# Moving the gate and up weight loads of the expert stage from SyncE's queue to ScalarE's

## The reference

```python
# first half, x is [4, 8192, 1024], H = 2048
xn = rms_scale * x / (norm + EPS) * split_scale
K = sigmoid(xn @ W_K)
u, g_in, g_out = split(xn @ W_ugg, 3)
u = u * sigmoid(g_in) * (1.0 - K)
outputs = scan(h[t] = K[t-1] * h[t-1] + u[t])
x = layernorm(x + outputs * sigmoid(g_out) @ W_out + x)
# second half, per token, E = 8 experts, F = 768
scores = sigmoid(x @ W_gate_router); top 2, normalised to w
shared = silu(x @ Wg_s) * (x @ Wu_s) @ Wd_s
routed = sum over the two of w * (silu(x @ Wg[e]) * (x @ Wu[e])) @ Wd[e]
x = layernorm(x + shared + routed)
```

## Time and profile before

| | us |
|---|---|
| median of 2 runs | 6612.8 (6410.53 and 6815.06) |
| the profiled execution | 6211.95 |
| its span on the slowest core, 7 | 6210.1 |
| spans of all cores | 6129.4 to 6210.1 |
| busy on core 7: TensorE matmul | 4513.6 (73%) |
| VectorE | 2209.9 (36%) |
| ScalarE | 901.8 (15%) |
| GpSimd | 482.8 (8%) |

### The profile page before, as it was taken

The page is one execution under the profiler, slowest core; times in us unless marked ns, Lnnn a source line. Parts: engine busy times, 40 slices in busy tenths (PEclk is TensorE's granted clock), DMA queues, the critical chain, the costliest instruction groups (busy, mean ns, idle before and its releaser), DMA issues.

```text
span 6210.1 us, 59657 instructions; the slowest of 8 cores (6129.4 to 6210.1 us)
## 1 busy us (share of the span) xinstructions
PE 4513.6 (73%) x19474; PEld 1886.0 (30%) x19474; DVE 2209.9 (36%) x3379; ACT 901.8 (15%) x1454; POOL 482.8 (8%) x433
## 2 busy tenths in 40 slices
PE   0000777878887878888598778887788877888797
PEld 0000233333333333333133333333333333333332
DVE  0000344444433333433234343443434434344333
ACT  0000112121221122221111111111111111111110
POOL 0000010010000000000300200102001020010000
PEclk9999899999989989889799989999899998999987
DMA  9999643443355442444432433324333243332331
GB/s 111 114 114 120 114 136 115 133 133 122 109 149 156 122 128 90 132 153 149 122 122 92 156 112 124 134 92 156 112 124 134 92 156 112 123 135 92 136 122 44
DMA packets 613866, 759.46 MB, mean 122 GB/s; under 512 B 140458, under 2 KB 525610, under 8 KB 611634
## 3 DMA queue, kind: packets, MB, share of 16 engines
q1 hardware_dynamic: 592658, 654.47, 32.8%
q0 software_dynamic: 20912, 101.19, 11.5%
HBM read 806.48 MB, written 88.60 MB: 144 GB/s over the span
## 4 chain that ended last, share of the span: by engine, by line
PE 59%; DVE 14%; another core or an unknown queue 10%; DMA 5%; issue 4%; ACT 4%; POOL 2%; DVEq 0%; SPq 0%; ACTq 0%; POOLq 0%
PE pb L694 12%; PE pb L700 12%; PE pb L731 11%; PE pb L490 8%; PE pb L481 4%; PE pb L511 3%; PE pb L472 3%; DVE AF L504 3%; PE pb L642 3%; DMA AB<-wout_bf 2%; DVE AF L499 1%; DVE AF L495 1%; DMA AB<-wugg_bf 1%; ACT AF L477 1%
## 5 line engine op out<-in xcount | busy, mean ns | idle before, releaser
L731 PE MATMUL pb<-AB 128*128 128x512 bf16 x3456 | 829.5, 400 | 306.9 <-DVE AF L737 113.0
L694 PE MATMUL pb<-AB 128*128 128x512 bf16 x3456 | 831.0, 384 | 12.4 <-ACT t L705 12.4
L700 PE MATMUL pb<-AB 128*128 128x512 bf16 x3456 | 830.2, 384 | 0.0
L472 PE MATMUL pb<-AB 128*128 128x512 bf16 x2048 | 522.6, 401 | 295.3 <-DMA AB<-wk_d 205.2
L495 DVE SCALAR_TENSOR_TENSOR AF<-pb,AF 128x512 f32<-128x512 f32 x256 | 177.0, 691 | 1413.7 <-PE pb L490 1413.7
L731 PEld LDWEIGHTS pb<-AB 128*128 128x128 bf16 x3456 | 343.5, 102 | 791.2 <-issue 517.4
L490 PE MATMUL pb<-AB 128*128 128x512 bf16 x2048 | 492.8, 384 | 106.0 <-ACT AF L477 105.9
L709 DVE TENSOR_TENSOR t<-t,pb 128x512 f32<-128x512 f32 x384 | 264.0, 687 | 812.4 <-PE pb L700 756.7
L481 PE MATMUL pb<-AB 128*128 128x512 bf16 x2048 | 504.9, 391 | 38.8 <-DMA AB<-wugg_bf 20.7
L741 DVE TENSOR_TENSOR AF<-AF,pb 128x512 f32<-128x512 f32 x512 | 351.8, 687 | 456.0 <-PE pb L731 377.0
L700 PEld LDWEIGHTS pb<-AB 128*128 128x128 bf16 x3456 | 341.4, 99 | 418.2 <-issue 42.0
(11 more groups left out here) (113 smaller groups left out, 2394.8 us busy)
## 6 DMA issues: line engine op xcount, KB each, us to landing
AB<-wugg_bf SPq DMA_DIRECT2D x152, 1024.0 KB, 8.8
AB<-wg_bf SPq DMA_DIRECT2D x72, 1536.0 KB, 6.7
AB<-wu_bf SPq DMA_DIRECT2D x72, 1536.0 KB, 9.4
AB<-wd_bf SPq DMA_DIRECT2D x72, 1536.0 KB, 7.4
AB<-wk_bf SPq DMA_DIRECT2D x60, 1024.0 KB, 5.8
xt<-xc SPq DMA_DIRECT2D x24, 2048.0 KB, 14.8
AB<-wout_bf SPq DMA_DIRECT2D x64, 512.0 KB, 4.7
o_core<-AF POOLq DMA_DIRECT2D x8, 2048.0 KB, 7.6
```

The costliest lines, as they stand in the source:

```text
L472: t.matmul(pA[:, :], wkq[:, kc * NT + m * 128: kc * NT + m * 128 + 128], xnb[:, kc * NT:(kc + 1) * NT], start=(kc == 0), stop=(kc == DC - 1))
L694: t.matmul(pA[:, :], wgbuf[:, kc * F + fc * 128: kc * F + fc * 128 + 128], x1b[:, kc * NT:(kc + 1) * NT], start=(kc == 0), stop=(kc == DC ...
L700: t.matmul(pB[:, :], wubuf[:, kc * F + fc * 128: kc * F + fc * 128 + 128], x1b[:, kc * NT:(kc + 1) * NT], start=(kc == 0), stop=(kc == DC ...
L731: t.matmul(pY[:, :], wdbuf[:, kc * 1024 + dc * 128: kc * 1024 + dc * 128 + 128], hbuf[:, kc * NT:(kc + 1) * NT], start=(kc == 0), stop=(kc ...
```

## The change

The `wg` and `wu` loads of the second stage are issued by ScalarE. The buffers, the semaphores' names, the waits and the place in the order of recording stay. `wd` and all other loads stay on SyncE. `emit` marks the semaphores of these loads as those of DMAs.

```diff
@@ -266,7 +266,8 @@
-        if eng in ("sync",) or (eng == "gpsimd" and n % 16 == 0 and n >= 16):
+        if (eng in ("sync",) or (eng == "gpsimd" and n % 16 == 0 and n >= 16)
+                or (eng == "scalar" and sem.startswith("lf"))):
             R.dma_sems.add(sem)
@@ -667,11 +668,11 @@
-            tok_wg = emit("sync", lambda sy, e=e, wgbuf=wgbuf: sy.dma_start(
+            tok_wg = emit("scalar", lambda sy, e=e, wgbuf=wgbuf: sy.dma_start(
                 wgbuf.rearrange("p (c f) -> p c f", f=F),
                 wg_bf.ap()[e * D:(e + 1) * D, :].rearrange("(c p) f -> p c f", p=128)),
                 outs=[b_wgb], sem="lfg" + str(par), n=16, extra=[tok_casts])
-            tok_wu = emit("sync", lambda sy, e=e, wubuf=wubuf: sy.dma_start(
+            tok_wu = emit("scalar", lambda sy, e=e, wubuf=wubuf: sy.dma_start(
                 wubuf.rearrange("p (c f) -> p c f", f=F),
                 wu_bf.ap()[e * D:(e + 1) * D, :].rearrange("(c p) f -> p c f", p=128)),
                 outs=[b_wub], sem="lfu" + str(par), n=16, extra=[tok_casts])
```

## The result

The changed kernel is slower by a ratio of 1.0191, with a 95% interval of 1.0161 to 1.022, beside a forecast of 1.017. The median over 13 runs is 6487.07 us (6297.45 to 6971.09), that of the kernel before over 10 runs 6572.48 us (6186.41 to 6815.06). The two medians point the other way than the ratio because in most executions of either kernel one die or both are held at a lower granted clock, by amounts that differ; the ratio takes the executions without that, three of 6304.7 us in the mean against two of 6186.7. The profiled execution took 6307.29 us, its span on core 7 was 6304.3 us: 94.2 more than that of the profiled execution before.

The account below looks back on a forecast made before the run. It took TensorE, busy 73% of a 6210.1 us span, as the bound. Late loads of expert 0 cost 103.6 us in tiles 1 to 7 and 3.2 in tile 0: 6612.8+107 = 6720 us, range 6300 to 6920.

Parts of the forecast that it names:

- What bounds: Whole kernel: TensorE, busy 73% of 6210.1 us; expert weights arrive in time, so an earlier load wins nothing.
- The ordinary expert, cost 0: 64 experts: loads leave after ScalarE's last Silu, some 13.5 us before the gates, and land 4 us early or more.
- rival 2: Gates of experts 2 to 8: each ordinary expert late too, 3.5 us each, 196 us; 6515 or 6916 us; chance 8%.
- Expert 0 of tiles 1 to 7, 14.8 us each: Tile starts: loads stand behind the LayerNorm's Exp, so expert 0 starts late; 103.6 us in all, bounds 81 to 126.
- rival 1: Tile starts: no change within 0.5%, the 13 us being taken back; 6212 or 6613 us; chance 7%.
- Expert 0 of tile 0, 3.2 us: First tile: loads move behind the router's Exp, handing over 3.2 us late; bounds 2 and 8.
- SyncE's queue, 0: wd, x and y alone on SyncE leave little earlier; value 0, bounds 0 and a gain of 1 us per tile.
- The sum, 107 us: Whole kernel: 103.6+3.2 us lost, between 83 and 134; 6319 us on the profile's footing, 1.7% more.
- The base: Whole kernel: the earlier runs' median, 6612.8 us, to which the loss was added unscaled for 6720 us.
- The clock as a gain: Expert stage: more idle time at tile starts lifts the granted clock; 6040 or 6441 us, 2.8% faster; chance 4%.

Follow-up runs that it names:

- experiment 1: Changed kernel, but expert 0's pair for tiles 1 to 7 issued right behind ScalarE's last Silu of expert 8, ahead of the LayerNorm's rows; ratio 1.0008.
- experiment 3: Kernel before, SyncE issuing everything, but wg and wu of expert 0 of tiles 1 to 7 also wait for ScalarE's LayerNorm Exp; ratio 1.0203.
- experiment 2: Changed kernel, but only expert 0's pairs of tiles 1 to 7 stay on ScalarE, the other 65 back on SyncE; ratio 1.027.
- experiment 7: Accumulator and squares tracked by chunks, in the kernel before (ratio 0.9877) and in the kernel of experiment 1 (0.988).
- experiment 5: Changed kernel, but y and expert 1's wd held until expert 0's wu has landed; first round no ratio, second 1.0159.
- experiment 6: Changed kernel plus 40, then 58 unread matmuls ahead of expert 0's gates in tiles 1 to 7; no ratio, periods 402.6 to 402.9 us with 58.
- experiment 4: The changed kernel measured again, nothing altered; ratio 1.0162.

## Why the prediction was right, step by step

- *What bounds.* Right: the only new waits are on the gates and ups of expert 0.
- *The ordinary expert, cost 0.* Right. The loads leave 14.1 us ahead and no gate waited; the kernel of experiment 1, with all 72 pairs on ScalarE, is at 1.0008. So rival 2 is out. Issue took ScalarE 0.37 and 0.55 us in its gap of 13.8.
- *Expert 0 of tiles 1 to 7, 14.8 us each.* Right in kind and nearly in size: 14.0 at the down matmuls and 13.7 in the period on core 0, 16.5 in the period on core 7. Experiments 1 and 3 show that the place behind the Exp is the cause, taken away and put in by itself. So rival 1 is out too: of 14.0 us late at the first down matmuls, 13.7 were still there at the next sums. That the size is so near is in part luck, as three terms inside were off and partly cancelled. First, the pair was said to leave at the end of the Exp, 8.4 us after the sums of squares; it left with its start, 7.8 after them. Second, the landings were too short, with most of y and wd said to have moved by then: wg was put at 6.7 us and took 7.6 to 8.2 on core 0 in tiles 1 to 6 and 7.6 to 11.1 on core 7; wu was put at 10.9 us behind the issue of wg and landed 11.5 to 12.1 behind it on core 0. Third, the ups were charged at half clock, 2.93 us, which puts 1.2 us on the clock. On core 0 they took 1.87 in the tile shown; on core 7 1.72 to 3.01. The term depends on how long wu lands behind wg, which the forecast did not ask. Relative to the sums of squares the forecast had the ups at +19.3 and the second gates at +22.2; core 0 had +19.7 and +21.5, core 7 +23.1 in the mean for the second gates.
- *Expert 0 of tile 0, 3.2 us.* Core 7 lost 3.2 us from the router's Exp to its sums.
- *SyncE's queue, 0.* Right for the changed kernel. That it mattered what SyncE puts beside the late pair was named only as a bound; experiment 2 shows how far it reaches.
- *The sum, 107 us.* Core 0 lost 101.6; a ratio of 1.0191 on 6186.7 us is 118, and one of 1.0162 would be 100.
- *The base.* The point, 6720 us, stood on the median of two runs. The median over ten was 6572, and the later medians of the kernel before were 6401, 6614 and 6202. The step was sized right and set on a base that scatters by more than it, so the median even fell. That the range held 6487 is no evidence for the mechanism: it was made as wide as the scatter. The evidence is the ratio and the waits.
- *The clock as a gain* (the third rival) did not show: in the profiled executions the mean granted clock was 0.917 to 0.923, against 0.919 to 0.929 before.
- The Trainium skill, "DMA: Bandwidth & Descriptors", section "Issuing engines are not separate DMA queues", says that issuing from several engines saves only the sequencer's issue time. Experiments 1 and 7 agree where the moment of issue is nearly the same (1.0008, and 0.988 against 0.9877). The loss of the change is one of the moment, of which that sentence says nothing.

## What to carry to other kernels

A DMA cost ScalarE little (0.37 and 0.55 us a pair, in an idle gap), but it inherits every wait that stands ahead of it in that engine's program. Before moving a load to a compute engine, look for the place where that engine waits for a result of the very engine that needs the load. Here it was the seam between two tiles: expert 8 and expert 0 share a buffer, and the kernel before issued wg for expert 0 of tiles 1 to 7 only 36.5 to 38.4 us ahead of its gates, against 47.3 or more for every other expert. And when a load is late, what the core's other queue has in flight adds to it, about 1 us for y and wd (experiment 5) and 6 to 11 us for three weight loads and y (experiment 2): keep loads that are not urgent behind it.

## What the runs showed of the hardware that I had not expected

- One pair of loads, issued 3 to 6 us behind four loads of 5632 KB together on another queue, landed in 16.9 and 22.4 us; in the last tile, without them, in 6.6 and 10.1 (experiment 2).
- The same load with nothing of its own core beside it took 6.6 to 6.9 us on one core and 9.0 to 9.7 on another in one execution (experiment 5). What the difference is stays open.
- The tile period did not follow small shifts: in tile 4, with the second gates at +20.99 (experiment 6, core 5), +21.54 (the changed kernel, core 0) or +22.24 (experiment 4, core 0), it was 402.8 to 402.9 us. Most periods fell on few values, 400.9, 402.8, 404.6 and some 406. Part of it is seen in experiment 6, where the wait of the down matmuls for VectorE's copy grew from 16.61 us on core 0 of the changed kernel to 17.02 on core 5 as the shift shrank. Another part is the granted clock behind pauses, as at the sums above. The rest was not followed.
